# Causal attention in one long kernel: the mask moves from TensorE to VectorE, the second pass takes several heads per product, and the side work gets new places

## What is computed

```python
# latent attention (16 heads of 8); the direct one has plain q, k, v of the same shapes
k_rope = k_rope * cos + rotate_half(k_rope) * sin          # "turned" keys, and so the queries
scores = jnp.einsum('bqhd,bkhd->bhqk', qq, kk) * scale
scores = jnp.where(causal[None, None], scores, finfo.min)   # the causal mask
probs = jax.nn.softmax(scores, axis=-1)
y = jnp.einsum('bhqk,bkhd->bqhd', probs, v).reshape(B, S, H)
```

## Time and profile before

| | value |
|---|---|
| median of 3 runs | 3226.27 us (3219.61 to 3237.03) |
| the profiled execution | 3232.98 us, its span 3231.2 us |
| mean granted TensorE clock | 0.919 of full speed |
| busy: PE, DVE, ACT, POOL | 81%, 67%, 44%, 36% |
| `mla` (first to last reduction) | 555 to 1348 us |
| `mha` (first to last reduction) | 1903 to 2649 us |

### The profile page before, as it was taken

One profiled execution on the slowest core, in us unless ns is written; L12 is line 12 of the kernel. 1 busy time (PEld: TensorE's weight loads), 2 busy tenths in 40 slices (PEclk: granted clock), 3 DMA queues, 4 the chain that ended last, 5 costly groups with the idle time before them and its releaser, 6 DMA issues. The chain is left out here.

```text
span 3231.2 us, 51537 instructions
## 1 busy us (share of the span) xinstructions
PE 2618.4 (81%) x17479; PEld 2011.4 (62%) x17479; DVE 2178.6 (67%) x5628; ACT 1414.6 (44%) x2412; POOL 1177.9 (36%) x2298
## 2 busy tenths in 40 slices
PE   1445873999999999948888759999999997698972
PEld 1423662777777777636666647777777766486861
DVE  5733773777777767448888846676767754677785
ACT  0001330455555555511111225666666652586861
POOL 3210110334434344322222113454455442773076
PEclk9997995899999999969999969999999995799996
DMA  2144001213223222031110032222122114697772
GB/s 29 32 134 127 23 13 30 41 29 44 42 29 47 37 34 41 15 104 50 49 49 32 3 43 33 31 40 36 25 40 40 26 17 165 231 296 225 250 218 73
DMA packets 198657, 228.02 MB, mean 71 GB/s; under 512 B 48621, under 2 KB 148814, under 8 KB 190478
## 3 DMA queue, kind: packets, MB, share of 16 engines
...
## 5 line engine op out<-in xcount | busy, mean ns | idle before, releaser
L1394 PE MATMUL banks<-Kb,Qb 96*128 96x128 f32 (+3 forms) x2048 | 599.6, 348 | 58.6 <-issue 27.3
L1406 PE MATMUL banks<-Qb,Kb 98*128 98x512 f32 (+3 forms) x2048 | 602.7, 356 | 4.8 <-ACT mha_prob L1297 1.0
L1101 DVE TENSOR_REDUCE mha_nm<-banks 128x1 f32<-128x384 f32 (+3 forms) x704 | 421.5, 639 | 185.9 <-PE banks L1398 172.3
L1101 DVE TENSOR_REDUCE mla_nm<-banks 128x1 f32<-128x384 f32 (+3 forms) x704 | 419.9, 638 | 160.0 <-PE banks L1398 146.5
L1297 ACT ACTIVATE mla_prob<-banks 128x512 f32<-128x512 f32 x640 | 376.5, 598 | 311.6 <-PE banks L1406 303.2
L1394 PEld LDWEIGHTS banks<-Kb,Qb 96*128 96x128 f32 x2048 | 364.3, 195 | 216.5 <-issue 159.9
L1297 ACT ACTIVATE mha_prob<-banks 128x512 f32<-128x512 f32 x640 | 375.7, 598 | 273.7 <-PE banks L1406 260.8
L1216 POOL TENSOR_SCALAR_AFFINE_SELECT mla_prob<-mla_prob 128x256 f32<-128x256 f32 (+1 forms) x640 | 237.8, 379 | 405.3 <-PE banks L1394 379.7
L1406 PEld LDWEIGHTS banks<-Qb,Kb 98*128 98x128 f32 x2048 | 334.8, 193 | 47.1 <-issue 7.6
L1216 POOL TENSOR_SCALAR_AFFINE_SELECT mha_prob<-mha_prob 128x256 f32<-128x256 f32 (+1 forms) x640 | 225.6, 361 | 355.4 <-PE banks L1394 329.2
L1828 PE MATMUL banks<-glu_wd,glu_hid 128*128 128x128 f32 x1024 | 147.7, 288 | 74.3 <-DVE glu_hid L1707 74.1
...
## 6 DMA issues: line engine op xcount, KB each, us to landing
...
Qb<-mla_qh SPq DMA_DIRECT2D x128, 64.0 KB
...
Qb<-mha_qh SPq DMA_DIRECT2D x128, 64.0 KB
```

Source lines behind the costliest of these rows:

```text
L1101: dve.tensor_reduce(nm[:, g % 2, h:h + heads, j], ps[:, bank1(g, k), 0:heads * w].rearrange("p (h k) -> p h k", h=heads), axis=AX.X, op=AL ...
L1394: one = pe.matmul(ps[:, bank, x * w:(x + 1) * w], Qb[0:MROW, u, g, h + x, j * P:(j + 1) * P], Kb[0:MROW, u, g, 0:w], start=(x == 0), stop= ...
L1406: last = pe.matmul(ps[:, S2 + k % 2, at:at + w], Kb[0:MROW + 2, u, grp, kb * P:(kb + 1) * P], Qb[0:MROW + 2, u, grp, h, kb * P:L], start=T ...
```

## The change

The causal mask is no longer a product. `mask` is a strip of 512 columns, zero but for the last 128, and VectorE adds it while it takes the maximum (`tensor_tensor_reduce`, which also writes its sum to an unused tile `junk`). The first pass has twelve units of one head: four of 512 columns, four of 384 + 128, four of 256, with a reduction for each row block, 16 a group. The second pass has eleven units with one product each: four of 512 columns, four of 384, and three in which two or four heads' narrower blocks fill 512 columns. `e_seen` is now given by PE's queue before the product. The sum that ends the turn and the low parts move from VectorE to GpSimd. The queries of `mla` are completed later in the slot, SyncE writes both kinds of query rows at g = 3 ahead of that group's maxima rows, and most other side work gets a new (g, k).

```diff
-UNITS1 = [(0, 0, HG)] + [(1, h, 2) for h in (0, 2)] + [(j, h, 1) for j in (2, 3) for h in range(HG)]
-UNITS2 = [u for a in (0, 2) for u in ([(a, 0, 0, L)], [(a, 3, 0, P), (a, 1, P, L - P)],
-                                      [(a + 1, 0, 0, L)], [(a + 1, 3, 0, P), (a + 1, 1, P, L - P)],
-                                      [(a, 2, 0, 2 * P), (a + 1, 2, 2 * P, 2 * P)])]
-WHERE = {(h, kb): (n, at, w) for n, unit in enumerate(UNITS2) for h, kb, at, w in unit}
-DIAGONALS = [sorted(at for _, _, at, _ in unit) for unit in UNITS2]
+UNITS = 3 * HG
+ROWS = [[(3, 0, L)], [(2, 0, 3 * P), (0, 3 * P, P)], [(1, 0, 2 * P)]]
+UNITS2 = [(0, h, 1) for h in range(HG)] + [(1, h, 1) for h in range(HG)] + [(2, 0, 2), (2, 2, 2), (3, 0, 4)]
+WIDE = [heads * (L - kb * P) for kb, _, heads in UNITS2]
+START = [sum(WIDE[:k]) for k in range(len(UNITS2))]
+WHERE = {(h + x, kb): START[k] + x * (L - kb * P) for k, (kb, h, heads) in enumerate(UNITS2) for x in range(heads)}
...
-        mask, identr = N.sb("mask", [P, HG, P], F32R), N.sb("identr", [P, P], F32R)
+        mask, junk = N.sb("mask", [P, L]), N.sb("junk", [P, 3, L], BF16)
         xs = N.sb("xs", [P, BLK, C])
         xth, xtl = N.sb("xth", [P, L], F32R), N.sb("xtl", [P, L], F32R)
         qh, ql, kh, kl = (N.sb(n, [P, L], F32R) for n in ("qh", "ql", "kh", "kl"))
-        tmp = N.sb("tmp", [P, L])
-        tmp2 = xs[:, :, :].rearrange("p b c -> p (b c)")
+        tmp, tmpq = N.sb("tmp", [P, L]), N.sb("tmpq", [P, L])
...
+        GATHER, VALUES_AT, OUT, SPLIT = 3, {5: (0,), 8: (1,), 10: (2, 3)}, 11, 9
+        TURNED = dict(pe=(0, 0), act=(0, 1))
+        DENSE = dict(pe=(0, 3), dve=(0, 5), add=((0, 8), (0, 10)), stats=(0, 7))
+        LATENTS = dict(pe=((0, 7), (0, 8)), act=(0, 9), dve=(0, 10))
+        if latent:
+            KEYS = dict(pe=((1, 0), (1, 6)), turn=(1, 7), add=(1, 8), act=(2, 0), low=(2, 2))
+            QUERIES = dict(pe=((2, 1), (2, 6)), turn=(2, 8), add=(2, 9), act=(3, 0), low=(3, 2))
+            NEXT_XS = dict(stats=(1, 2), rms=(1, 5), scale=((2, 4), (2, 6)))
+        else:
+            KEYS = dict(pe=((1, 0),), act=(1, 2), low=(1, 4))
+            QUERIES = dict(pe=((2, 1),), act=(2, 3), low=(2, 5))
+            NEXT_XS = dict(scale=((2, 7), (2, 8), (2, 9), (2, 10)))
+        VALUES = dict(pe=(3, 1), act=(3, 3))
+        NEXT = dict(pe=(3, 6), act=(3, 7), dve=(3, 9))
...
+                        if g == 3 and turn != "last" and proj:
+                            queries(1 - u)
                         if has_maxima(turn, g):
 
                             par, grp, to = (g + 1) % 2, (g + 3) % NG, u if g else 1 - u
                             sp.wait_ge(ml_ready, c.next(ml_ready))
                             sp.dma_start(f32(Qb[MROW:MROW + 2, to, grp, :, :]),
                                          f32(mhl[:, par, :])).then_inc(m_rows[par], 16)
-                        if g == 2 and turn != "last" and proj:
-                            queries(1 - u)
...
+                def row_maxima(g, k):
+                    h = k % HG
+                    dve.wait_ge(s1_ready, c.next(s1_ready))
+                    for j, at, w in ROWS[k // HG]:
+                        last = dve.tensor_tensor_reduce(junk[:, k % 3, at:at + w], ps[:, bank1(k), at:at + w], mask[:, L - w:L], -1.0,
+                                                        BIG, ALU.add, ALU.min, nm[:, g % 2, h, j:j + 1])
+                    last.then_inc(s1_free, 1)
...
+                def add_turned(parts, full, whole, product):
+                    pool.wait_ge(parts, c.next(parts))
+                    pool.tensor_tensor(whole[:, :], whole[:, :], product[:, :], ALU.add).then_inc(full, 1)
+
+                def low_part(high, whole, hi, lo, split_done):
+                    pool.wait_ge(high, c.next(high))
+                    pool.tensor_tensor(lo[:, :], whole[:, :], f32(hi[:, :]), ALU.subtract).then_inc(split_done, 1)
+
+                K_PART, Q_PART = (k_high, tmp, kh, kl, k_split), (q_high, tmpq, qh, ql, q_split)
...
                             if k == SPLIT and turn != "last":
                                 split_maxima(g % 2)
-                            if prep and g == NEXT_XS["g"]:
-                                if latent and k == NEXT_XS["rms"]:
-                                    inverse_rms()
-                                if k in NEXT_XS["scale"]:
-                                    prepare(n + 2, NEXT_XS["scale"].index(k))
-                            if dense and g == 1 and latent and k in DENSE["add"]:
-                                add_residual(n - 2, DENSE["add"].index(k))
+                            if prep and latent and at == NEXT_XS["rms"]:
+                                inverse_rms()
+                            if prep and at in NEXT_XS["scale"]:
+                                prepare(n + 2, NEXT_XS["scale"].index(at))
+                            if proj and latent and at == KEYS["add"]:
+                                add_turned(k_parts, k_full, tmp, sines)
+                            if proj and latent and at == QUERIES["add"]:
+                                add_turned(q_parts, q_full, tmpq, sines)
+                            if proj and at == KEYS["low"]:
+                                low_part(*K_PART)
+                            if proj and at == QUERIES["low"]:
+                                low_part(*Q_PART)
...
-                def scores(g, u, k, seen):
-
-                    j, h, heads = UNITS1[k]
-                    w = P * (j + 1)
-                    bank = bank1(g, k)
-                    back = 1 if g == 0 and k < 2 else 0
-                    pe.wait_ge(s1_free, c.next(s1_free) + back)
-                    for x in range(heads):
-                        one = pe.matmul(ps[:, bank, x * w:(x + 1) * w], Qb[0:MROW, u, g, h + x, j * P:(j + 1) * P],
-                                        Kb[0:MROW, u, g, 0:w], start=(x == 0), stop=False, skip_group_check=True)
-                        if seen and x == 0:
-                            one.then_inc(e_seen, 1)
-                    pe.matmul(ps[:, bank, 0:heads * w].rearrange("p (x w) -> p x w", x=heads)[:, :, w - P:w],
-                              identr[:, :], mask[:, 0:heads, :], start=False, stop=True,
-                              skip_group_check=True).then_inc(s1_ready, 1)
-
-                def scores_less_max(grp, u, k):
...
+                def scores(g, u, k):
+
+                    h = k % HG
+                    pe.wait_ge(s1_free, c.next(s1_free))
+                    for j, at, w in ROWS[k // HG]:
+                        last = pe.matmul(ps[:, bank1(k), at:at + w], Qb[0:MROW, u, g, h, j * P:(j + 1) * P],
+                                         Kb[0:MROW, u, g, 0:w], start=True, stop=True)
+                    last.then_inc(s1_ready, 1)
+
+                def scores_less_max(g, grp, u, k):
+
+                    kb, h, heads = UNITS2[k]
                     pe.wait_ge(s2_free, c.next(s2_free))
-                    for h, kb, at, w in UNITS2[k]:
-                        last = pe.matmul(ps[:, S2 + k % 2, at:at + w],
-                                         Kb[0:MROW + 2, u, grp, kb * P:(kb + 1) * P],
-                                         Qb[0:MROW + 2, u, grp, h, kb * P:L], start=True, stop=True)
-                    last.then_inc(s2_ready, 1)
+                    pe.sem_inc(e_seen, 1)
+                    pe.matmul(ps[:, bank2(g, k), 0:WIDE[k]].rearrange("p (x w) -> p x w", x=heads),
+                              Kb[0:MROW + 2, u, grp, kb * P:(kb + 1) * P],
+                              Qb[0:MROW + 2, u, grp, h:h + heads, kb * P:L], start=True, stop=True).then_inc(s2_ready, 1)
```

353 lines of the change are left out of this document (167 added, 186 removed).

## The result

The changed kernel takes 3415.4 us (median of 4 runs, 3406.6 to 3427.2) against 3226.4 beside it: ratio 1.0585, 95% interval 1.0539 to 1.0631. A second measurement gave 3421.4 against 3223.3, 1.0609 (1.0575 to 1.0643). The forecast said 3288, with 3375 as its upper end: right in the sign and the place, 127 us short in size.

A forecast was written before the change was run, and what follows sets the result against it. PE, 97 to 98% busy, was taken as the bound, VectorE next. `mla` +108, `mha` -42, last slots -12, starts +4 gave +58 on 3233.0: 3291, left as 3288; range 3160 to 3375, the forecast's own 3250 to 3345.

The forecast's parts named there:

- late queries in `mla`: Group 3 to next slot: query rows come late, PE starts 20 us after group 3 began, idle some 8 us.
- the longest waits: Sign: PE waits 7 to 9 us at group 0 of each `mla` slot; none over 3 us in `mha`.
- Behind a gap of 8 us I put in 2.0: `mla`, behind PE's wait for queries: half clock costs 2.0 us a slot, bounds 1.5 and 3.
- Groups 0 and 1 keep half of what the engines save: Groups 0 and 1 fall from 26.4 to 23.1 us in `mla` and to 21.0 in `mha`.
- together 1.8 us a group, 7.2 us a slot: PE in both attentions: work saved by dropping mask products and by the new second pass.
- The 1.08 us for the mask: PE, first pass: the eleven mask products of a group cost 1.08 us in all, which is saved.
- the 0.72 us for the second pass: PE, second pass: a group's products fall from 3.12 to 2.40 us.
- can't be shorter than 12.1: `mla` group 2: late key transfers and the maxima rows behind them keep it at 12.1 us or more, from 11.8.
- 8 us a slot more: VectorE: masked reductions and their 16 result writes, 8.1 us a group against 6.1, add 8 us a slot.
- nearly in time: Rival, `mla` group 3: `q_split` at about 4.5 us, rows nearly in time, 3184 us; chance 0.23 shared with 3040.
- VectorE as a bound: Rival, both attentions: dearer result writes and columns add 4 to 6 us a slot on VectorE; 3380 us; chance 0.12.
- its 3040 for that case: Both attentions, transfers no bound at all: slots of 43.5 and 41 us, 3040 us; shares the chance 0.23.

The follow-up runs named there:

- e1: Changed kernel with dummy products on PE while it waits for query rows, output unchanged; 115.6 us above the kernel before, ratio 1.0346.
- e9: Changed kernel repaired: old side-work places and SyncE order, additions on VectorE, low parts on GpSimd, slot loop written out; ratio 0.9684 to the kernel before.
- e6: e3 with the mask added by PE again and plain maxima on VectorE; ratio 1.0038 to the kernel before.
- e7: e3 with one second-pass product per head again, 16 a group in place of 11; ratio 0.9979 to the kernel before.
- e5: Changed kernel with additions and low parts of both attentions back on VectorE, late places kept; ratio 1.0235 to the kernel before.
- e3: Changed kernel with side-work places, SyncE's order, additions and low parts as before; new reductions and second pass kept; ratio 0.9875 to the kernel before.

## Why the prediction was wrong

Its mechanism stands: late queries in `mla` decide, and the run is slower. Its working of them held: the first transfer 6.15 us into group 3 (6.6), 14.9 us to PE's start (13.2), group 3 20.6 to 21.0 (20), the keys 4.6 us into group 2 (4.9), GpSimd's sum 1.28 us (1.3), `q_split` in `mha` 9.8 us into group 2 (10.3). The sum was short by 5.2 us in each slot: `mla` 62.4 against 57.2, `mha` 49.7 against 44.5. Twice 15 slots are 156 us; the measured median is 127 us above the forecast, since the slots before were a little longer than the 50.0 and 47.3 us that I started from, the first and last slots lost less than the middle ones, and the profiled run is 12 us above its median. (3291 less 7 is also 3284 and not 3288.) Of its signs, the longest waits stand where it put them, but with 4.4 to 6.6 us in place of 7 to 9, and `mha` has 3.59 us where none over 3 was to be. These steps failed.

**The clock: "Behind a gap of 8 us I put in 2.0", and nothing in `mha`.** It was taken from 3 us at half clock behind one gap of the convolution. In the attentions the clock stays at 0.50 for some 10 us behind most waits, behind one of 2.66 us too, so also at group 3 and in `mha`. What it costs is shown by e1: 3.4 us a mean slot in `mla` and 2.6 in `mha`, 4 us more for the two together than I had. The 2.7 us between the slots of `mha` with long and with short low stretches say the same. The Trainium skill ("TensorE: Matmul & The Clock Gate", HAM oscillation) has the rule that a burst of products behind a DMA wait starts cold; the rows agree, and show it for both waits of an `mla` slot.

**What the free groups gain: "Groups 0 and 1 keep half of what the engines save".** They were to fall from 26.4 to 23.1 us in `mla` and from 24.0 to 21.0 in `mha`; with the low clock gone, in e1, they take 24.5 and 22.7. Behind it stands "together 1.8 us a group, 7.2 us a slot". PE's busy time over 14 slots is 49.0 us a slot in `mla` and 46.5 in `mha` before, and 45.3 and 42.9 in e9: 3.7 and 3.6 us less. (Busy time is modelled at its ends, but the short `mha` slots fall by as much, from 47.3 to 43.7.) The 1.08 us for the mask are near what e6 shows (0.8 to 0.9), but the 0.72 us for the second pass came from start-to-start times within one group, and e7 shows 0.1 to 0.2. The rest in `mla` is waits: PE waits in e9 for VectorE's reductions and turned products 32.9 us over 14 slots, before 14.7.

**Groups 2 and 3.** In `mla` group 2 "can't be shorter than 12.1", and is 13.1: PE waits 2.63 us at its end for the maxima row behind the keys; e5, without GpSimd's addition and low part in front of the keys, has 1.1. Group 3 is 0.6 to 1.0 us over its 20. In `mha` the two take 24.2 to 24.6 us where I had 23.5.

**VectorE: "8 us a slot more".** It is some 2 by the pitch of the reductions, since the result write is hidden. This error doesn't show in the time: I had both engines at 42 to 44 us in `mla` and 40 to 41.5 in `mha`, VectorE too high and PE too low, and the pace that is left without late rows, some 48 and 43.7 us in the short slots of e3, is mostly PE's.

So for `mha` the 5.2 us are 2.6 for the clock and 2.6 for the groups; for `mla` they are 1.4 for the clock, 1.4 for groups 0 and 1, 1.0 for group 2 and 0.4 for group 3 by e1's best slots, and 1.0 by which e1's mean slot is longer than those.

The rivals: nearly in time fell by the first condition it named, `q_split` at 6.15 and not 4.5 us. VectorE as a bound is no part of after, where it is 57% busy, and only a small one of the repaired kernel; its condition, dearer result writes and columns, wasn't met. What the prediction didn't see is how much the change holds if the rows are in time; its 3040 for that case was too low, 3123 was reached, with the loop written out.

Left open: what of the 127 us belongs to clock and what to pace is known only within some 20 us, since e1's dummy products left some low stretches; why the low stretch behind waits of one length is 3.6 us in one place and 10 in another; and the low clock that before shows twice in `mla` without a wait for rows.
